# Histogram of a graph's degrees at another pace, and a second attention's table lookups with one-hots in place of a mask product

## The reference, cut to what matters

```python
h = jnp.maximum(_layernorm(x), 0.0)
x = x + _L0_gnn_ref(h, src, dst, edge_weight, ...)     # twice: gelu(ln((x + A x) @ W + b)), then a projection
h = jnp.maximum(_layernorm(x), 0.0)
x = x + _L1_gnn_ref(h, ..., src, dst)                  # gat_conv (8 heads), elu, gat_conv (1 head)

def gat_conv(x, W, attn_l, attn_r, src, dst, n_nodes):
    H, D = attn_l.shape
    feat = (x @ W).reshape(n_nodes, H, D)
    el = jnp.einsum('nhd,hd->nh', feat, attn_l)
    er = jnp.einsum('nhd,hd->nh', feat, attn_r)
    e = jax.nn.leaky_relu(el[src] + er[dst], 0.2)
    m = jax.ops.segment_max(e, dst, num_segments=n_nodes)
    ex = jnp.exp(e - m[dst])
    denom = jax.ops.segment_sum(ex, dst, num_segments=n_nodes)
    alpha = ex / denom[dst]
    out = jax.ops.segment_sum(alpha[:, :, None] * feat[src], dst, num_segments=n_nodes)
    return out.reshape(n_nodes, H * D)
```

## Time and profile before

| | us |
|---|---|
| median of 3 runs | 3194.01 |
| lowest, highest | 3188.41, 3195.47 |
| the profiled execution, whole time | 3189.21 |
| its span | 3187.4 |

### The profile page before, as it was taken

The page is one execution under the profiler, slowest core; times in us unless marked ns, Lnnn a source line. Parts: engine busy times, 40 slices in busy tenths (PEclk is TensorE's granted clock), DMA queues, the critical chain, the costliest instruction groups (busy, mean ns, idle before and its releaser), DMA issues.

```text
span 3187.4 us, 53896 instructions
## 1 busy us (share of the span) xinstructions
PE 2625.3 (82%) x19041; PEld 1999.0 (63%) x19041; DVE 2339.0 (73%) x3630; ACT 1274.2 (40%) x3089; POOL 1000.2 (31%) x1235
## 2 busy tenths in 40 slices
PE   4666666788998999968689999787777778776999
PEld 3666666444454555558678888665555556665888
DVE  7999999677523444367899999997777777325886
ACT  7777777101000111110045555465555554203443
POOL 3000000011110222240047777777777773002000
PEclk8989999899999999989899999999999999758999
DMA  4444334533346777441167777777777773441553
GB/s 140 164 166 166 155 158 166 213 98 100 116 157 206 245 259 245 147 154 46 38 176 224 226 222 224 191 222 218 217 217 217 217 217 116 133 128 51 166 160 111
DMA packets 310840, 541.17 MB, mean 170 GB/s; under 512 B 108465, under 2 KB 213187, under 8 KB 310323
## 3 DMA queue, kind: packets, MB, share of 16 engines
q1 hardware_dynamic: 241426, 312.45, 29.7%
q0 software_dynamic: 69152, 225.28, 24.4%
HBM read 423.70 MB, written 115.11 MB: 169 GB/s over the span
## 4 chain that ended last, share of the span: by engine, by line
PE 67%; DVE 20%; issue 5%; ACT 4%; POOL 2%; DMA 2%; DVEq 0%; POOLq 0%; SPq 0%; ACTq 0%
PE ps L1574 24%; PE ps L1360 14%; PE ps L1562 9%; PE ps L1496 8%; DVE a L547 6%; DVE a L543 3%; PE ps L1494 3%; PE ps L1274 2%; DVE a L544 2%; PE ps L1329 2%; DVE a L762 2%; PE ps L1388 1%; ACT oht L1243 1%; PE ps L1331 1%; PE ps L1332 1%
## 5 line engine op out<-in xcount | busy, mean ns | idle before, releaser
L1360 PE MATMUL ps<-a 128*128 128x512 f32 x1200 | 578.3, 613 | 14.8 <-DMA a<-at_d 13.9
L1574 PE MATMUL ps<-a,oh 128*128 128x260 f32 x2008 | 489.5, 391 | 86.2 <-issue 47.3
L1683 POOL DMA_INDIRECT a<-t,srci x502 | 479.2, 955 | 216.6 <-issue 137.8
L1243 ACT ACTIVATE oht<-iota,ndl 128x128 f32<-128x128 f32 x830 | 333.3, 402 | 445.9 <-PE ps L1574 404.4
L1574 PEld LDWEIGHTS ps<-a,oh 128*128 128x128 f32 x2008 | 365.2, 190 | 191.5 <-issue 87.4
L1329 PE MATMUL ps<-a 128*128 128x200 bf16 x1568 | 326.1, 267 | 165.9 <-DVE a L543 80.9
L1574 PE MATMUL ps<-wts,oh 128*128 128x260 f32 x1312 | 320.1, 391 | 55.0 <-ACT oh L1245 31.9
L1059 DVE TENSOR_TENSOR a<-a,ps 128x520 f32<-128x520 f32 x502 | 325.8, 691 | 49.5 <-DMA a<-t,srci 46.8
L1683 POOL DMA_INDIRECT wts<-t,srci x328 | 313.7, 956 | 108.3 <-issue 92.5
L1360 PEld LDWEIGHTS ps<-a 128*128 128x128 f32 x1200 | 216.1, 195 | 194.9 <-issue 192.4
L1633 POOL TENSOR_SCALAR rstd<-mv 128x1 f32<-128x1 f32 x75 | 22.9, 305 | 1004.0 <-DVE mv L442 1001.7
(11 more groups left out here) (321 smaller groups left out, 4327.6 us busy)
## 6 DMA issues: line engine op xcount, KB each, us to landing
a<-at_d SPq DMA_DIRECT2D x60, 1280.0 KB, 6.1
at_d<-a SPq DMA_DIRECT2D x49, 800.0 KB, 3.3
mt_d<-a SPq DMA_DIRECT2D x49, 800.0 KB, 5.3
a<-mt_d SPq DMA_DIRECT2D x30, 1280.0 KB, 6.0
a<-trlo_d SPq DMA_DIRECT2D x49, 512.0 KB
ot_d<-a SPq DMA_DIRECT2D x49, 320.0 KB, 5.6
a<-ot_d SPq DMA_DIRECT2D x49, 320.0 KB, 3.2
a<-t,srci POOLq DMA_INDIRECT x502, 3.7
```

Source lines behind the costliest of these rows:

```text
L1243: e.activation(oht[:, k, :], iota[:, :], ACT.Abs, bias=ndl[:, k, s:s + 1]).then_inc(*own.inc())
L1360: m = e.matmul(acc[f].rearrange("p (x d) -> p x d", x=8), X[:, hi, P * f:P * (f + 1)], a, start=(hi == 0), stop=False, skip_group_check=True)
L1574: t = e.matmul(pbig[b][:, 512 * u:512 * u + 260], oh[:, so, k, :], hrows[2 * r + k][:, 260 * u:260 * (u + 1)], start=(k == 0), stop=(k == 1))
L1683: e.indirect_dma_start(out=hrows[2 * r + k], out_offset=None, in_=t2, in_offset=bass.IndirectOffsetOnAxis(ap=srci[:, k, s:s + 1], axis=0)) ...
```

## The change

Two parts, which have nothing to do with each other.

1. **Histogram.** DVE's part of group g moves from step `2 + 2g` to step `2 + 9g // 4` (the last one from 98 to 110), and PE's part becomes a job of its own, `histogram product`, two steps later (the last one at 112).
2. **Lookups of the second attention.** PE leaves the mask product out: three matmuls per column instead of four. DVE no longer takes a maximum. It builds a one-hot of each edge's block (`source_block`, 16 x 25, bf16), multiplies PE's result with it (from PSUM into SBUF) and sums the 25 values. `source_block` of group g+1 stands ahead of the multiplication of group g. The place in PSUM is free (`found`) after the multiplication. The loads from `ot_d` shrink from 320 to 256 KB. To have the blocks, SP loads the sources again (`src2`, three DMAs at the end of the heads' loop), and DVE shifts and converts them (2 instructions of 128x782) ahead of block 6 of the elu stage. The table of minus 1e30 is no longer built for this stage, so that its first load and first matmul no longer wait for it.

```diff
 for g_ in range(NG):
-    JOBS.setdefault(2 + 2 * g_, []).append(("histogram", g_))
+    JOBS.setdefault(2 + 9 * g_ // 4, []).append(("histogram", g_))
+    JOBS.setdefault(4 + 9 * g_ // 4, []).append(("histogram product", g_))
...
-                e.tensor_copy(tv[2], r).then_inc(*V.inc())
+                e.tensor_copy(tv[2], r).then_inc(*V.inc(("look", H)))
+                if H == 1:
+                    return
...
-                for i, (g, q, m, _) in enumerate(LOOKUPS[1]):
-                    found(1, i, el2[:, 16 * g + q:16 * g + q + m, :])
+                def source_block(g):
+                    m = min(16, J - 16 * g)
+                    e.tensor_tensor(ohh2[:, g % 2, 0:m, :], every(iotab[:, 0:NB], m), col(hib2[:, 16 * g:16 * g + m], NB), ALU.is_equal).then_inc(*V.inc())
+                source_block(0)
+                for g in range(NG):
+                    m = min(16, J - 16 * g)
+                    if g + 1 < NG:
+                        source_block(g + 1)
+                    e.wait_ge(pe_look, LOOK0[1] + g + 1)
+                    e.wait_ge(*V.last())
+                    e.tensor_tensor(picked[:, g % 2, 0:m, :], pbig[g % 3][:, 0:512].rearrange("p (t w) -> p t w", w=32)[:, 0:m, 0:NB], ohh2[:, g % 2, 0:m, :],
+                                    ALU.mult).then_inc(*V.inc(("found", 1, g)))
+                    e.wait_ge(*V.last())
+                    e.tensor_reduce(el2[:, 16 * g:16 * g + m, 0], picked[:, g % 2, 0:m, :], AX, ALU.add).then_inc(*V.inc())
...
+                if name == "elu" and b == 6:
+                    e.wait_ge(src2_in, 48)
+                    e.tensor_scalar(src2, src2, 7, None, ALU.arith_shift_right).then_inc(*V.inc())
+                    e.wait_ge(*V.last())
+                    e.tensor_copy(hib2, src2).then_inc(*V.inc())
...
-                    e.matmul(pp[:, k, 0:W], ot[0:100, 16 * P + P * c:16 * P + P * (c + 1)], nbf[0:100, (q + k) % 4, :], start=True, stop=False)
+                    if H == 8:
+                        e.matmul(pp[:, k, 0:W], ot[0:100, 16 * P + P * c:16 * P + P * (c + 1)], nbf[0:100, (q + k) % 4, :], start=True, stop=False)
                     for z in range(3):
-                        t = e.matmul(pp[:, k, 0:W], ot[:, (q + k) * P:(q + k + 1) * P], tbl[:, z, 0:W], start=False, stop=(z == 2))
+                        t = e.matmul(pp[:, k, 0:W], ot[:, (q + k) * P:(q + k + 1) * P], tbl[:, z, 0:W], start=(H == 1 and z == 0), stop=(z == 2))
...
+                w = GW if H == 8 else 16 * P
+                e.dma_start(ots[H][g % n][:, 0:w], ot_d[:, GW * g:GW * g + w]).then_inc(ot_in[H][g % n], 16)
...
+            natural(src2, src, src2_in)
```

More of the change, by code:

```diff
@@ L333, in program @@
         mx2 = a1f[:, 1000:1000 + J].rearrange("p (j h) -> p j h", h=1)
+        src2 = a1f[:, 2100:2100 + J].bitcast(I32)
+        hib2 = a1f[:, 2900:2900 + J // 2].bitcast(BF16)
+        ohh2 = a1f[:, 3300:3700].bitcast(BF16).rearrange("p (u j d) -> p u j d", u=2, j=16)
+        picked = a1f[:, 3700:4500].rearrange("p (u j d) -> p u j d", u=2, j=16)
         mxn, rn, els = (small[:, 256 + 64 * i:256 + 64 * i + w] for i, w in ((0, NB), (1, 2 * NB), (2, 2 * NB)))
@@ L360, in program @@
         sc_out, hl_in, exs_out = (sem(n) for n in ("sc_out", "hl_in", "exs_out"))
-        mx_out, mxn_in, msmall_in = (sem(n) for n in ("mx_out", "mxn_in", "msmall_in"))
+        mx_out, mxn_in, msmall_in, src2_in = (sem(n) for n in ("mx_out", "mxn_in", "msmall_in", "src2_in"))
         mpiece_in = [sem(f"mpiece_in{u}") for u in range(NPC)]
@@ L1415, in job @@
                 kind = name if isinstance(name, str) else name[0]
-                if kind == "histogram":
+                if kind == "histogram product":
                     g = name[1]
@@ L1835, in one_hots_back @@
                     e.wait_ge(pe_look, LOOK0[H] + LAST_OF[H][g - n] + 1)
-                e.dma_start(ots[H][g % n], ot_d[:, GW * g:GW * (g + 1)]).then_inc(ot_in[H][g % n], 16)
+                w = GW if H == 8 else 16 * P
+                e.dma_start(ots[H][g % n][:, 0:w], ot_d[:, GW * g:GW * g + w]).then_inc(ot_in[H][g % n], 16)
             LAST_OF = {H: [i for i, (_, _, _, end) in enumerate(LOOKUPS[H]) if end] for H in (8, 1)}
```

## The result

| | before | changed |
|---|---|---|
| median | 3192.44 us (3188.41 to 3195.47, 4 runs) | 3155.38 us (3154.72 to 3156.54, 4 runs) |
| profiled execution | 3189.2 us | 3155.9 us |
| span of the trace | 3187.4 us | 3154.1 us |

The ratio is 0.9885 (95% interval 0.9872 to 0.9897): the change makes the kernel 37 us faster. Measured again in a later session it gave 3156.68 us and 0.9881 (0.9866 to 0.9896). Forecast were 3156 us and a range of 3138 to 3180.

The account below looks back on a forecast made before the run. PE was taken as the bound, waiting for DVE's one-hots and slowed by its clock, and pacing the lookups. Part one's 29.4 us plus part two's 9.1 gave 38.5 us less, a median of 3156 us, range 3138 to 3180.

Parts of the forecast that it names:

- Where PE waits: First convolution: 25.9 us of PE waits at 19 places shrink to one to six places, under 6 us in all.
- The clock: First convolution: the lower clock costs 10.2 us of PE's work, of which 2.5 us would remain.
- Is there enough DVE?: Histogram: at nine steps for four groups, DVE needs 109.4 us against PE's 118.7 over 54 steps.
- DVE stays late: First convolution, rival: DVE may not regain its two-step lead; part one gains 15 us, total 3170 us; chance 0.16.
- The lookups' period: Lookups: DVE's three instructions and gaps take 1.76 us per group, 76.3 us from group 5 to the scan.
- the rival of the fast one-hot: Lookups: DVE's one-hot takes 0.2 us less, period 1.56 us, gain 8.6 us larger, 3147 us; chance 0.08.
- The bound of the lookups: Lookups: DVE at 1.76 us per group becomes the bound, above PE's 1.47 us for 48 matmuls.
- Start and elu: Lookups' start gains 1.6 us by lighter loads and no table; two elu-stage instructions cost 1.1 us.
- nothing covers them: Elu stage: DVE's two new instructions cost their full 1.1 us, since DVE and ACT take turns on one chain.
- The loads of `src2`: End of the heads' loop: three loads issued some 40 us ahead of use cost nothing.
- Nothing was given back: End of first convolution, rival: saved time is waited for at a gather; part one worth nothing, 3185 us; chance 0.08.
- nothing ran in turn: Lookups, rival: PE and DVE alternate, period 2.75 us; 3212 us with half of part one's gain; chance 0.04.

Follow-up runs that it names:

- The lead alone: Kernel before with PE's histogram product two steps later, still one group per two steps: 3164.6 us, ratio 0.9905.
- one maximum: Changed kernel whose lookups take one DVE maximum per group, with no mask and no one-hots (wrong values): 3143.26 us, ratio 0.9838.
- POOL and ACT: Changed kernel with the lookups' one-hots made by POOL (subtract) and ACT (Abs, Relu) instead of DVE: 3141.04 us, ratio 0.9827.
- an early one-hot: Changed kernel with 15 of the 49 groups' one-hots built in the elu stage, where DVE waits for ACT: 3149.06 us, ratio 0.9849.

## Why the prediction was right, point by point

**Where PE waits** was right. 4.3 us at three places stand against a forecast of "under 6 us at one to six places", and the sizes I left (2.2 us behind the scans and 2.0 for the count jobs) came as 2.5 and 1.9. Idle time went down by 21.9 us, forecast 21.7. The lower bound was not worked out well: half of the 36.1 us is 18, not 15.

**The clock** was nearly right, and a term beside it was missing. I took 10.2 us from a mean of 0.96 over 255 us and left a quarter, so 7.7 gained; the work at the lower level says 8.3. PE's busy time fell by 11.1, and the other 2.8 us, what PE loses at each wait besides the idle time, weren't in my sum. Part one so gained 33.0 us where the sum had 29.4, near the upper bound of 34; alone it gained 34.8, just above it, in an execution in which the clock didn't fall at the wait that is left.

**"Is there enough DVE?"** was the step that carried no weight. I took the nine steps for four groups to be a condition of the gain. The lead alone brings 31 us, at the old pace. My own figures said so (117.4 us of DVE against 120.0 of PE), and I drew the new pace into the argument anyway. The runs show that the lead of two steps was enough. The rival "DVE stays late" falls with it: DVE waits for PE at seven places, 23.8 us.

**The lookups' period** was right to the hundredth, 1.76 us, and 76.5 us from group 5 to the scan against 76.3. The nearest rows for each instruction and the three gaps of rows 5 and 7 were enough, and each of them came as forecast (0.61, 0.49 and 0.67 us from start to start). The one-hot takes 0.57 us (0.56 to 0.57 for 400 bf16 elements), so the rival of the fast one-hot falls. What I held against it was half of a rule. The page "VectorE: DVE Perf Modes" of the Trainium skill gives a bf16 `tensor_tensor` in SBUF twice the speed in its section "The perf-mode tier table", but its section "What auto-detection actually checks" asks for a step of 1 or -1 on every tensor. The block of an edge is read here 25 times in a row, with a step of 0, and 0.57 us is what the trace has for 400 elements in f32 too, so the two agree. By the section "The DRAIN you can't avoid" of the same page of the Trainium skill, which finds no cost of a semaphore after each operation, the gaps would not grow with the waits. Here they do (-0.08, 0.04 and 0.10 us with none, one and two), and 1.72 us was not reached.

**The bound of the lookups** was right, DVE over PE, and so was PE's side as a mean: 1.47 us per group with one maximum, and 13 us of room under DVE where I wrote 12.5, of which POOL and ACT had 12. What I didn't see is what the mean is made of, 1.21 to 1.28 us and stalls. PE's idle time from group 5 on was ended by DVE as forecast for 7.8 us, and 2.4 us of it were such stalls.

**Start and elu.** Table to scan gained 10.1 us, forecast 8.6 + 1.6 = 10.2: 8.4 from group 5 on and 1.7 before it. That is closer than the traces allow. From group 5 to the scan the unchanged lookups took 84.9 us in the profile before and 85.9 to 87.4 in three others, so that the gain there is 8.4 to 10.9 us. The elu stage shows its two new instructions ahead of block 6:

```profile
2665.00 0.69 DVE L1114 SCALAR_TENSOR_TENSOR a<-a 128x512 f32<-128x512 f32 x1 [0.69 <-ACT a L1280]
2665.61 0.56 DVE L1103 TENSOR_SCALAR a<-a 128x782 int32<-128x782 int32 x1
2666.21 0.57 DVE L1105 CAST a<-a 128x782 bf16<-128x782 int32 x1
2666.69 0.69 DVE L1107 TENSOR_TENSOR a<-a,den 128x512 f32<-128x512 f32 x1
```

From 2665.61 to 2666.69 are 1.08 us that stand between no other blocks; forecast 1.1. That "nothing covers them" was true of the place only: an early one-hot of 0.57 us cost nothing where DVE waits for ACT, so these two would likely fit there as well, one per block. No run tried it.

**The loads of `src2`** I had at nothing, because they are issued some 40 us ahead of use. Their use didn't wait, but they cost some 2 us at the end of the heads' loop. I asked when they are needed and not what else is on its way then. In part two's sum the cost was thus too small by 2 us and, against most traces, the gain too small by as much.

**Nothing was given back** behind the histogram, and nothing ran in turn. The chain there moved with PE: what was saved in the convolution is there in the end.

**The total** was hit with help. Against the profiled execution I forecast 38.5 us less and 33.3 came, though the stages I had sized won 42.0 us (33.0 + 10.1 - 1.1), 3.5 more than forecast. Of the missing 8.7 us 7.8 are the unchanged start. Against the median, 37.1 us, these errors nearly cancel, and that the median was hit within 1 us is luck: the runs of one kernel alone spread by 2 to 13 us.

## What to carry to other kernels

Where two engines work in step and one of them has its work in lumps, look at how far ahead the producer may be before looking at how much it has to do: here a lead of two steps was worth 31 us and 11% fewer groups per step nothing by themselves. A wait of the matmul engine can cost more than it lasts: 21.9 us less of idle time came with 11.1 us less of busy time, 8.3 of them by the clock. Compare busy times for the same instructions to see it, and the work in the stretches at the lower clock to tell the clock's part. A load that nobody waits for isn't free: ask what it shares the DMA engines with (here some 2 us). When a change makes another engine the bound (1.76 us of DVE over PE's mean of 1.47), add up what idle engines could take over: here POOL and ACT, idle in that stage, gave 12 us more in it.

## What the runs showed of the hardware

An unchanged stage isn't the same from run to run. In thirteen traces, with the same instructions in it, the first product came between 583.7 us (before) and 591.5 (changed). From the second convolution to the table the time was 1770.4 to 1773.0 us in the four kernels without part two and 1773.8 to 1780.1 in the nine with it; some 3 us of that are the change, and up to the piece with the new loads the same instructions spread over 7 us. PE's own busy time moves with it; the stretch from 50 to 583 us of the kernel before, then of the changed one (PE, clock, DMA, GB/s):

```profile
50.00:583.00 533.00, 349.77 (x4723) 0.89 0.40 159
```
```profile
50.00:583.00 533.00, 361.12 (x4723) 0.87 0.39 155
```

The same 4723 rows, with a clock of 0.87 instead of 0.89. The kernel with one maximum, the same as the changed one up to there, worked 348.5 us. What decides it the traces don't show. It means that a difference of two profiled executions should be read stage by stage.

The clock hardly matters to the small matmuls. Two stretches of the kernel with one maximum, each the length of a group of 48 matmuls in which PE never stood still (start:end, length, PE, clock, DMA, GB/s):

```profile
2747.40:2748.60 1.20, 1.20 (x54) 1.00 0.63 167
2721.70:2723.00 1.30, 1.30 (x56) 0.50 0.88 271
```

At the clock's upper level DVE's rows stand 1.21 us apart (2747.38 and 2748.59), at the lower one 1.28 (2721.69 and 2722.97): 25 and 27 ns for a matmul of 25 columns. In the kernels with 64 matmuls per group it is 1.60 and 1.71 us. Half the clock costs 6% there. With f32 products of 512 columns in the convolution it costs its full share: their rows follow each other by 0.43 us at the upper level and by 0.85 at the lower (711.3 to 714.7 us of the kernel before).
